# Values times exponentials as three half-precision products in a decoder's cross-attention

## The reference

```
kv  = concat(layer_norm(context) (154 rows), layer_norm(x) (512 rows))   # 666 rows
q, k, v = xn @ Wq, kv @ Wk, kv @ Wv
out = softmax(q @ k.T * 0.125) @ v         # 512 x 666 per head
x   = layer_norm(x + concat_heads(out) @ Wo)
```

## Time and profile before

| what | value |
|---|---|
| median of three runs | 1936.24 us |
| profiled execution, its own time | 1942.76 us |
| its span, first to last instruction | 1941.0 us |
| PE busy | 1681.8 us, 87% of the span |
| DVE busy | 1112.8 us, 57% |
| ACT busy | 704.9 us, 36% |
| POOL busy | 594.6 us, 31% |
| mean granted PE clock, of full speed | 0.917 |

### The profile page before, as it was taken

One profiled execution on the slowest core, in us unless ns is written; L12 is line 12 of the kernel. 1 busy time (PEld: TensorE's weight loads), 2 busy tenths in 40 slices (PEclk: granted clock), 3 DMA queues, 4 the chain that ended last, 5 costly groups with the idle time before them and its releaser, 6 DMA issues.

```text
span 1941.0 us, 39582 instructions
## 1 busy us (share of the span) xinstructions
PE 1681.8 (87%) x17094; PEld 844.0 (43%) x17094; DVE 1112.8 (57%) x2186; ACT 704.9 (36%) x1039; POOL 594.6 (31%) x648
## 2 busy tenths in 40 slices
PE   5888877779999999998979977989989898869996
PEld 1222223223334334333225446767777675643443
DVE  6778675775565465465245664554556642452555
ACT  1766554334443443443422322433424331221120
POOL 1000000343354633563520045466444660000000
PEclk9989888799999999999979998998999997967698
DMA  3000002223322332222201023312233121100000
GB/s 133 1 1 1 1 12 78 63 63 88 87 63 78 86 89 63 75 76 56 61 12 57 1 23 56 57 34 36 48 57 56 34 39 30 45 1 0 6 6 11
DMA packets 132909, 86.56 MB, mean 45 GB/s; under 512 B 105578, under 2 KB 106671, under 8 KB 132480
## 3 DMA queue, kind: packets, MB, share of 16 engines
q1 hardware_dynamic: 99456, 79.85, 16.4%
q10 hardware_dynamic: 33280, 4.20, 1.4%
HBM read 55.12 MB, written 28.90 MB: 43 GB/s over the span
## 4 chain that ended last, share of the span: by engine, by line
PE 57%; DVE 25%; POOL 6%; issue 5%; DMA 3%; ACT 3%; SPq 1%; ACTq 0%; POOLq 0%; DVEq 0%
PE ps L153 55%; DVE a_MX L357 4%; DVE b_mx L811 3%; POOL d_XI L1521 3%; POOL d_tmp L1518 2%; DVE st L159 1%; PE ps L213 1%; DVE sq L192 1%; POOL b_SUM L878 1%; DVE d_KV L1494 1%; DVE st L174 1%; DMA d_G<-s_g 1%; SPq L162 1%; DVE st L185 1%; DVE b_rd L956 1%
## 5 line engine op out<-in xcount | busy, mean ns | idle before, releaser
L811 DVE TENSOR_REDUCE b_mx<-ps 128x2 f32<-128x666 f32 x256 | 217.5, 850 | 172.6 <-PE ps L153 172.5
L878 POOL TENSOR_TENSOR b_SUM<-b_SUM,b_E 128x1024 f32<-128x1024 f32 x96 | 228.5, 2380 | 36.8 <-ACT b_E L865 25.0
L1518 POOL TENSOR_TENSOR d_tmp<-d_G,d_XI 128x31 f32<-128x31 f32 (+15 forms) x248 | 127.1, 512 | 331.1 <-DMA d_G<-s_g 312.3
L865 ACT ACTIVATE b_E<-ps 128x1024 f32<-128x1024 f32 x160 | 164.0, 1025 | 177.1 <-PE ps L153 177.1
L878 POOL TENSOR_TENSOR b_SUM<-b_E,b_E 128x1024 f32<-128x1024 f32 x32 | 75.4, 2357 | 349.3 <-PE ps L153 281.4
L153 PE MATMUL ps<-b_M,b_S 128*128 128x512 f16 (+1 forms) x768 | 178.6, 388 | 1.4
L357 DVE TENSOR_REDUCE a_MX<-ps 128x2 f16<-128x1024 f32 x128 | 154.9, 1226 | 39.8 <-PE ps L153 39.8
L153 PE MATMUL ps<-b_E,b_V 128*64 128x512 f32 x640 | 173.8, 622 | 1.4 <-ACT b_OT L156 0.8
L394 ACT ACTIVATE a_E<-ps 128x1024 f32<-128x1024 f32 x128 | 131.2, 1025 | 95.5 <-PE ps L153 95.3
L1521 POOL TENSOR_TENSOR d_XI<-d_XI,d_tmp 128x31 f32<-128x31 f32 (+15 forms) x248 | 140.9, 568 | 19.4
L153 PE MATMUL ps<-b_Hk,b_Hq 64*128 64x333 f16 x512 | 82.9, 320 | 32.9 <-DVE b_mx L811 30.8
(11 more groups left out here) (303 smaller groups left out, 3023.1 us busy)
## 6 DMA issues: line engine op xcount, KB each, us to landing
b_S<-s_xk SPq DMA_DIRECT2D x48, 336.0 KB, 6.3
b_M<-s_xq SPq DMA_DIRECT2D x48, 256.0 KB, 5.1
s_xk<-b_Hk SPq DMA_DIRECT2D x16, 336.0 KB, 2.2
s_xk<-b_Lk SPq DMA_DIRECT2D x16, 336.0 KB, 2.3
s_xq<-b_Hq SPq DMA_DIRECT2D x16, 256.0 KB, 2.0
s_xq<-b_Lq SPq DMA_DIRECT2D x16, 256.0 KB, 2.0
d_XI<-eye SPq DMA_DIRECT2D x8, 512.0 KB, 4.2
s_g<-d_L ACTq DMA_DIRECT2D x32, 128.0 KB, 4.5
```

What stands on the lines that cost most here:

```text
L811: v.e.tensor_reduce(out, PS[:, bk:bk + 2, 0:333], AX, ALU.max).then_inc(sem("b_mx"), 1)
L865: a.e.activation(b_E[k % 6], PS[:, bk:bk + 2, :], ACT.Exp, scale=0.125).then_inc(sem("b_ex"), 1)
L878: p.e.tensor_tensor(b_SUM[a], x, b_E[k % 6], ALU.add).then_inc(sem("b_sum"), 1)
L1518: e.tensor_tensor(tm, a, x, ALU.mult).then_inc(*p.step())
```

## The change

The exponentials and the values are kept as two f16 parts, high and low, and their product is made as three f16 products: high by high, low value by high exponential, high value by low exponential. The denominators come from the same parts.

- ACT: Exp now writes a float32 tile `b_X` (two of them), and a second instruction copies it to an f16 tile `b_EH` (six). The Exp into a `b_X` waits until POOL has read that tile two slots before. The remainder has `b_XR`, `b_RH`.
- POOL: its additions go. It writes the low parts `b_EL` = `b_X` - `b_EH` instead, ten of 1024 elements and one of 512 (`b_RL`) in a unit.
- PE: a values slot is three pairs of f16 matmuls in place of a pair of float32 ones, and waits for POOL's low part in place of ACT's Exp. The denominators come in three groups, in slots 5 and 9 of the unit and slot 4 of the next, of 16 f16 matmuls each.
- DVE: value projections get low parts too (`b_VL`, three in a unit), and there are three additions to `b_den` in a unit, not one. In each slot the addition and the projection's low part now come ahead of both maxima; the low part stood between them.
- Items 4 and 8 move: the table of items is now {0, 1, 2, 3, 4, 6, 7, 8, 10}. The side work of ACT and DVE starts one slot later. The layout of SBUF and three semaphores' sharing follow.

```diff
             if s < 10:
                 k = 10 * u + s
+                o, w = (k - 2) // 10, (k - 2) % 10
+                a.wait_ge("b_el", 11 * o + w + 1)
+                a.e.activation(b_X[k % 2], PS[:, bk:bk + 2, :], ACT.Exp, scale=0.125).then_inc(sem("b_ex"), 1)
                 o, w = (k - 6) // 10, (k - 6) % 10
                 a.wait_ge("b_pv", 11 * o + w + 1)
-                a.wait_ge("b_sum", 8 * o + (w - 2 if w > 1 else w) + 1)
-                a.e.activation(b_E[k % 6], PS[:, bk:bk + 2, :], ACT.Exp, scale=0.125).then_inc(sem("b_ex"), 1)
+                a.wait_ge("b_dm", 3 * o + w // 4 + 1)
+                a.wait_ge("b_ex", n + 1)
+                copy(a.e, b_EH[k % 6], b_X[k % 2]).then_inc(sem("b_eh"), 1)
...
+        def b_low_gpsimd(p, u, s):
+            p.wait_ge("b_eh", 11 * u + s + 1)
+            if s < 10:
+                k = 10 * u + s
+                last = p.e.tensor_tensor(b_EL[k % 6], b_X[k % 2], b_EH[k % 6], ALU.subtract)
...
-                for par in range(2):
-                    last = mm(e, PS[64 * par:64 * par + 64, 6 + a, :], V[:, 4 * c + 2 * a + par, :], b_E[(10 * u + s) % 6][:, par, :],
-                              start=(c == 0), stop=False)
+                for V, E, first in ((H, b_EH[k], True), (L, b_EH[k], False), (H, b_EL[k], False)):
+                    for par in range(2):
+                        last = mm(e, PS[64 * par:64 * par + 64, 6 + a, :], V[:, 4 * c + 2 * a + par, :], E[:, par, :],
+                                  start=(c == 0 and first), stop=False)
...
+            t.wait_ge("b_el", 11 * u + min(4 * c + 4, 11))
+            for s in range(4 * c, min(4 * c + 4, 10), 2):
+                for E in (b_EH, b_EL):
+                    for j in range(4):
+                        last = mm(e, PS[32 * j:32 * j + 32, bk, :], b_one[:, g, :], E[(10 * u + s + j // 2) % 6][:, j % 2, :],
+                                  start=(s == 4 * c and E is b_EH), stop=False)
...
-        B_ITEM = {0: 0, 1: 1, 2: 2, 3: 3, 5: 4, 6: 5, 7: 6, 8: 7, 9: 8}
+        B_ITEM = {0: 0, 1: 1, 2: 2, 3: 3, 4: 4, 6: 5, 7: 6, 8: 7, 10: 8}
+        B_DEN = {5: (0, 0), 9: (0, 1), 4: (1, 2)}
...
             mx = b_maxima(u, s)
+            if b_part(x - 1):
+                b_den_vector(v, *b_part(x - 1))
+            if b_item(x - 1):
+                b_project_vector(v, *b_item(x - 1))
             if mx:
                 b_max_vector(v, *mx)
-            if u + 2 < NU and s - 1 in B_ITEM and s < 8:
-                b_project_vector(v, u + 2, B_ITEM[s - 1])
-            if mx:
                 b_max_vector(v, mx[0], mx[1] + 1)
```

More of the change, by code:

```diff
@@ L633, in build @@
         b_M1, b_M2 = [b_four(f"b_M1{k}", 1024) for k in range(2)], [b_four(f"b_M2{k}", 1024) for k in range(2)]
-        b_V = [rB.take(f"b_V{k}", 1344).rearrange("p (c n) -> p c n", n=64) for k in range(3)]
+        b_VH = [rB.take(f"b_VH{k}", 672, F16).rearrange("p (c n) -> p c n", n=64) for k in range(3)]
+        b_VL = [rB.take(f"b_VL{k}", 672, F16).rearrange("p (c n) -> p c n", n=64) for k in range(3)]
         b_Hq = [rB.take(f"b_Hq{k}", 512, F16).rearrange("p (a n) -> p a n", a=2) for k in range(2)]
@@ L750, in b_project_scalar @@
                 w = 512 if k < 8 else 320
-                last = copy(e, b_V[u % 3][:, c:c + w // 64, :], PS[:, bk, 0:w].rearrange("p (c n) -> p c n", n=64))
+                last = copy(e, b_VH[u % 3][:, c:c + w // 64, :], PS[:, bk, 0:w].rearrange("p (c n) -> p c n", n=64))
             last.then_inc(sem("b_pc"), 1)
@@ L758, in b_project_vector @@
             v.wait_ge("b_pc", 9 * u + k + 1)
-            v.wait_ge(f"b_w{(u - 1) % 2}", 64 * ((u + 1) // 2))
-            if k < 2:
+            if k < 6:
+                v.wait_ge(f"b_w{(u - 1) % 2}", 64 * ((u + 1) // 2))
+            if k > 5:
+                c, w = 8 * (k - 6), 512 if k < 8 else 320
+                last = e.tensor_tensor(b_VL[u % 3][:, c:c + w // 64, :], PS[:, bk, 0:w].rearrange("p (c n) -> p c n", n=64),
+                                       b_VH[u % 3][:, c:c + w // 64, :], ALU.subtract)
+            elif k < 2:
                 last = e.tensor_tensor(b_Lq[:, k, :], PS[:, bk, :], b_Hq[i][:, k, :], ALU.subtract)
@@ L961, in b_out_vector @@
             e.tensor_tensor(b_rp[:, 1, :], b_rd, b_rp[:, 0, :], ALU.subtract).then_inc(sem("b_rt"), 1)
-            for _ in range(3):
+            for _ in range(2):
                 yield
@@ L968, in b_out_vector @@
                 yield
+            yield
             v.wait_ge("b_out", b + 1)
@@ L1009, in b_side_vector, with b_item, b_part @@
                 yield from later(44 - B_OUT, ())
-        B_ITEM = {0: 0, 1: 1, 2: 2, 3: 3, 5: 4, 6: 5, 7: 6, 8: 7, 9: 8}
+        B_ITEM = {0: 0, 1: 1, 2: 2, 3: 3, 4: 4, 6: 5, 7: 6, 8: 7, 10: 8}
+        B_DEN = {5: (0, 0), 9: (0, 1), 4: (1, 2)}
+        def b_item(x):
+            u, s = x // 11, x % 11
+            return (u, B_ITEM[s]) if 0 <= u < NU and s in B_ITEM else None
+        def b_part(x):
+            u, s = x // 11 - 2, x % 11
+            if s not in B_DEN or not 0 <= u - B_DEN[s][0] < NU:
+                return None
+            return u - B_DEN[s][0], B_DEN[s][1]
         def b_maxima(u, s):
@@ L1093, in b_gpsimd @@
             for u in range(NU):
-                b_sum_gpsimd(p, u)
+                for s in range(11):
+                    b_low_gpsimd(p, u, s)
         def b_sync(s):
```

106 lines of the change are left out of this document (53 added, 53 removed).

## The result

Four runs of the changed kernel took 1967.09 to 1984.74 us, median 1978.83, against 1932.60 to 1936.55, median 1935.45, for before. The ratio estimated from the runs is 1.0185, 95% interval 1.0132 to 1.0238 (the medians divide to 1.0224). Slower, as forecast, and inside the range; the time forecast, 1966, is 13 us short of the median. The profiled execution took 1975.23 us (span 1973.4), where the prediction's sum for it was 1972.6.

A forecast was written before the change was run, and what follows sets the result against it. PE and a 1.27 us DVE floor coincide as limits. Terms +19.5 + 9.3 + 6 - 5 = +29.8 give 1972.6 us from the profiled 1942.76; 6.5 down to the median, 1966. Own range 1948 to 1985; 8 in 10: 1938 to 1990.

The forecast's parts named there:

- The floor of 1.27 us: First to second maxima block, through DVE: 0.36 + 0.85 + 0.06; shorter values gain 0 in eight slots.
- Rival 1: PE's work is what counts: unit changes by -1.3 us, whole 1913 us; chance 0.08.
- Values 0.77 us: Three f16 pairs in a values slot, 0.24 less than before; gained only in slots 5 to 7, -0.72 a unit.
- Denominators: Three groups on PE, uncovered behind the second block or in slot 5: 3.3 us for 1.99, +1.3 a unit.
- The low part ahead of the maxima: DVE's reductions start later: +0.14 in slot 1, +0.13 in slot 9, +0.6 in slot 8; together +0.87 a unit.
- The unit: Steady unit of the stage: -0.72 + 1.3 + 0.87 - 0.06 = +1.4 us, fourteen times, +19.5 us.
- Rival 2: Floor holds, the rest is hidden: ACT in time in slot 8, layer norms in POOL's gaps; 1938 us, chance 0.13.
- End of a sequence: Three times: reciprocal and `b_rp` nearer slot 8's maxima, about +1.1, layer norm about 2; +3.1 each, +9.3 us.
- The end of the stage: From slot 5 of unit 14 POOL paces, 45 us for 48.98: -4; slot 4's denominators -0.9; together -5 us.
- The start: 280 to 440 us, DVE-bound: six low parts 3.7, two denominators 1.4, ports about 1; +6 us, bounds 0 and 15.
- POOL near 26 us a unit: POOL's low parts in a unit: 10 x 2.48 + 1.2 = 26 us; values' matmuls keep 0.5 us to spare.
- Rival 3: POOL starves PE, values wait in slots 6 to 8: +14 + 17, 1997 us; chance 0.13.

The follow-up runs named there:

- r2: Changed kernel without the product of the values' low part with the exponentials' high part, two pairs a slot for three; median 1974.95 us, before 1936.14.
- r4: Changed kernel with PE's projection block put ahead of the second maxima block in all slots with maxima; median 1971.75 us, before 1936.14.
- r6: Kernel before with the projection block ahead of the second maxima block in the 22 first slots and steady units; median 1945.33 us, ratio to before 1.0024.
- r3: Changed kernel whose denominators sum the exponentials' high parts alone; median 1959.96 us, before 1936.14.
- r11: Changed kernel with DVE's low part of query and key blocks, not values, between its two maxima in all slots; 1965.69 us in one run.
- r8: Changed kernel without the low part of the reciprocals of a sequence's denominators, the high part taken twice; 1985.37 us in one run.

## Why the prediction was right, and where a size was off

- The floor of 1.27 us and its consequence, no gain in the eight slots with maxima: right, by the trace, by r2 and by r4 and r6 from two sides. Rival 1 is out.
- Values 0.77 us: measured 0.77; slots 5 to 7 gave what was said (slot 6 went from 2.63 to 2.40 us).
- Denominators: on the path, as said (r3), but 1.08 + 0.98 + 0.87 = 2.93 us and not 3.3, 0.24 us a set, the lower of my two rows. +0.94 for +1.3.
- The low part ahead of the maxima: slots 1, 8 and 9 are the right ones; from block to block they are 1.38, 1.74 and 1.37 us long, +0.68 in all for +0.87. Slot 2 was said to be covered, and took no more than in before (1.38 for 1.39); r11 shows that without the low part it would be 1.27.
- The unit: +0.98 for +1.4. Fourteen of them are 13.7 us for 19.5, 5.8 less. Rival 2, which put the unit at +0.5, is out: slot 8 waits 0.66 us, and the layer norms did not fall into POOL's gaps.
- End of a sequence: four units grew from 159.4 to 166.7, 3.9 as units and 3.4 extra, for 3.1 predicted; the reciprocal's chain has 1.6 of it (r8), predicted 1.1. The third time the extra was 5.6, 1.5 of it by the clock, which the prediction left out; so 12.4 us in all for 9.3. The reciprocal itself did not get dearer (3.34 us for 3.35), the cast behind it did (1.42 for 0.93), the subtraction not (2.62 for 2.73).
- The end of the stage: -4.8 for -5, and the 5.95 us wait is gone, as said. But the price was right in part by luck. The terms listed add up to 45.6 us and not 45, and POOL, said to pace this stretch, doesn't: from slot 5 of unit 14 to stage three (976.99 to 1021.53, 44.5 us) PE is busy for 38.5 us and POOL for 36.2, and PE waits 2.4 us for POOL and 3.5 for ACT. A low part takes 2.13 us and not 2.48.
- The start is the term that was mis-sized: 13.5 us up to the first row alone, for 6 in all of 280 to 440 us (bounds 0 and 15). The next three steps gave 0.9 of it back beside their unit's term, so about 12.6 are left. I counted what DVE gets to do, low parts and denominators, and not what it has to wait for. In slot 1 I followed the low part through ACT's queue and found 0.14 us; in the first slots the same queue has stage one's exponentials in it, and the low part waits 2.02 us and more. That PE's clock may fall with such waits stood in the bound and not in the value.
- POOL near 26 us a unit: 22.45, since a low part takes 2129 ns and not 2480. Rival 3 is out: the values waited for POOL six times in the stage, 2.4 us in all, every time after 985 us, and never in the steady unit.

The forecast's mechanism was right, its sum for the profiled run (1972.6 for 1975.23) close by misses of opposite sign, which is luck: the unit came out 5.8 us low, the start some 7 and the ends 3 high, and stage three, whose code is the same, took 2.5 us less than in before's profile. The step to the median, 6.5 us down, had no ground for another kernel: the profiled run of the changed one lies 3.6 below its median. The upper end of the forecast's own range, 1985, mixes the two: with +2.3 a unit the terms give +42.5 us, 1979 from the median and 1985 only from the profiled time.

## What to carry to other kernels

When two engines pass a buffer to and fro, lay out both gaps of the cycle and compare each with the round trip: work taken out of a gap at the floor gains nothing, work moved from a long gap into a short one gains, and the same move costs where the short gap was full. When an instruction is moved ahead of another on its engine, price it in every stretch of the program with the queue that its producer has there, the first slots above all. Where an untouched stage varies by 25 us from run to run, date events in the changed stage instead of comparing totals.

## What was not expected of the hardware

- POOL's subtraction of f16 from float32 into f16, 128x1024, takes 2129 ns, its float32 additions 2.48 us apiece when they follow each other; the two-input f16 addition, 1159 for 512, had led me to expect no difference. For 512 elements the subtraction takes 1158.
- DVE's cast of 512 elements from SBUF took 428 ns when POOL was idle and 1416 in the middle value of four, the subtraction beside it 691 and 2622 (by tile, the changed kernel: ns min/median/max):

```profile
L986 DVE CAST b_rp<-b_rd x4: 428/1416/1423, 558.2 to 1035.7; 128x512 f16<-128x512 f32 x4
L988 DVE TENSOR_TENSOR b_rp<-b_rd,b_rp x4: 691/2622/2628, 559.6 to 1036.1; 128x512 f16<-128x512 f32 x4
```

- The granted clock between 286 and 349 us was anything from 0.71 to 0.83 for the same instructions; the first rows of these four profiles lie 9 us apart, the later the lower the clock.
- After the same wait of 2.28 us the clock stayed at 1.00 at one end of a sequence and fell to 0.66 over 5 us at another, which made the unit 1.5 us longer.
